# First feed-forward stage of an eight-stage kernel: side work dealt out anew over the four chunks of a unit

## What is computed

```python
def _L0_ffn_ref(x, Wg, ln_scale, ln_bias, W1, b1, W2, b2):   # x is _layernorm(x)
    logits = xt @ Wg.T
    top1 = jnp.argmax(logits, axis=-1)
    xhat = (xt - mu) * jax.lax.rsqrt(var + LN_EPS)
    def body(y, p):
        h = jax.nn.gelu((xhat * s_e + b_e) @ w1 + bb1, approximate=False)
        out = h @ w2 + bb2
        mask = (top1 == eid)[:, None].astype(out.dtype)
        return (y + mask * out, None)
```

## Time and profile before

| | us |
|---|---|
| median of 3 runs | 3491.15 |
| lowest, highest | 3480.52, 3493.16 |
| profiled execution, device time | 3460.41 |
| its span, first to last instruction | 3458.1 |
| the stage `f0`, first up step to the last combine | about 388 to 541 |

### The profile page before, as it was taken

How to read it: one execution, slowest core, us unless ns; L and a number is a source line. 1 busy time by engine, 2 the same in 40 slices (tenths; PEclk the granted TensorE clock), 3 DMA queues, 4 the chain that set the end, 5 groups by cost and what they waited for, 6 DMA issues and landing times. The chain is left out here.

```text
span 3458.1 us, 70868 instructions
## 1 busy us (share of the span) xinstructions
PE 2853.0 (83%) x26206; PEld 1911.0 (55%) x26206; DVE 2008.3 (58%) x4613; ACT 1670.4 (48%) x3112; POOL 1267.8 (37%) x1503
## 2 busy tenths in 40 slices
PE   5888576888879999999969889999209977999993
PEld 3544354445436666666645556666209865777772
DVE  4777454787655444443358777777724335555647
ACT  3777332666634444444337666666315533333331
POOL 6554005777300000000055455653260035555533
PEclk8999797999979999999979999999559978999995
DMA  3221002111124000000011111111142333333211
GB/s 112 70 70 58 13 1 75 61 63 61 33 66 159 1 1 1 1 1 1 6 56 60 61 48 39 43 45 31 41 167 87 93 98 85 81 84 83 65 29 49
DMA packets 211341, 190.00 MB, mean 55 GB/s; under 512 B 41840, under 2 KB 189568, under 8 KB 210848
## 3 DMA queue, kind: packets, MB, share of 16 engines
q1 hardware_dynamic: 184384, 167.44, 16.0%
q0 software_dynamic: 26624, 18.04, 2.0%
HBM read 67.09 MB, written 41.42 MB: 31 GB/s over the span
## 5 line engine op out<-in xcount | busy, mean ns | idle before, releaser
L1545 DVE TENSOR_TENSOR f1H<-f1HF,f1H 128x512 bf16<-128x512 f32 x256 | 176.6, 692 | 398.3 <-ACT f1H L1390 398.3
L1323 PE MATMUL ps<-f1xT,f1w 128*128 128x512 bf16 x1536 | 378.3, 383 | 6.1 <-ACT f1H L1390 6.1
L1345 PE MATMUL ps<-f1w,f1H 128*128 128x256 bf16 x3072 | 378.6, 273 | 0.0
L1345 PEld LDWEIGHTS ps<-f1w,f1H 128*128 128x128 bf16 x3072 | 301.0, 98 | 90.9 <-issue 1.1
L1387 ACT ACTIVATE f1HF<-ps 128x512 f32<-128x512 f32 x256 | 152.8, 597 | 333.9 <-PE ps L1323 333.8
L734 ACT ACTIVATE a2PT<-ps 128x512 f32<-128x512 f32 (+1 forms) x512 | 262.3, 542 | 100.9 <-PE ps L573 56.0
L430 POOL DMA_DIRECT2D a2QS<-a2MH x256 | 135.5, 535 | 289.1 <-DVE a2MH L959 276.4
L550 PE MATMUL ps<-a2KS,a2QS 49*128 49x256 bf16 (+1 forms) x1024 | 182.5, 269 | 69.4 <-DVE a2NM L853 24.5
L1323 PEld LDWEIGHTS ps<-f1xT,f1w 128*128 128x128 bf16 x1536 | 147.9, 98 | 151.1 <-issue 16.4
L1233 POOL TENSOR_TENSOR f1RS<-f1VE,neghalf 128x4 f32<-128x4 f32 x8 | 8.1, 1012 | 541.5 <-DVE f1VE L1528 541.5
L853 DVE TENSOR_REDUCE a0NM<-ps 128x2 f32<-128x512 f32 x256 | 166.2, 684 | 53.1 <-PE ps L550 52.8
(11 more groups left out here) (512 smaller groups left out, 7266.3 us busy)
## 6 DMA issues: line engine op xcount, KB each, us to landing
a2KS<-a2KH SPq DMA_DIRECT2D x192, 64.0 KB
a2QS<-a2QH SPq DMA_DIRECT2D x192, 64.0 KB, 2.6
a4KS<-a4KH SPq DMA_DIRECT2D x96, 128.0 KB
a4QS<-a4QH SPq DMA_DIRECT2D x96, 128.0 KB, 2.6
slots<-zeros SPq DMA_DIRECT2D x1, 9984.0 KB, 32.4
f2XS<-slots SPq DMA_DIRECT2D x39, 256.0 KB, 2.9
results<-f2XS SPq DMA_DIRECT2D x39, 256.0 KB, 2.1
f1WF<-in_f_w SPq DMA_DIRECT2D x32, 256.0 KB, 2.7
```

The source lines that it names most:

```text
L1323: m = nc.tensor.matmul(ps[:, (u * NCH + i) % 2, :], w1[:, x, kt, i * P:i * P + P], xT[:, half, y, kt, :], start=(j == 0), stop=(j == len(t ...
L1345: m = nc.tensor.matmul(out, H[:, (u * NCH + i) % HR, x, t * P:t * P + P], w2[:, y, i, :], start=first, stop=(f == YC - 1 and j == 2 and no ...
L1545: nc.vector.tensor_tensor(H[:, (u * NCH + i) % HR, 1, :], HF[:, (u * NCH + i) % 2, :], H[:, (u * NCH + i) % HR, 0, :], SUB).then_inc(S["h_ ...
```

## The change

In `f0` the side work of a unit is dealt out over its four chunks in another way:

| after chunk | before | after |
|---|---|---|
| 0 | xT 0 | xT 0, xT 1 |
| 1 | xT 1, route | route, gate |
| 2 | stats, gate | stats |
| 3 | apply, sel | sel, apply |

xT, route, gate and sel are those of the next unit, stats and apply those of the unit after it. In addition the four DVE multiplications of the ties by a triangular mask (L1443, one per tile) become one over all four tiles. The order of `f1` stays as it was.

```diff
         def early(u, k):
-            k = k if paired else k // 2
+            if paired:
+                if u + 1 < UNITS:
+                    yield from ((("xT", u + 1, 0), ("xT", u + 1, 1)), (("route", u + 1, 0), ("gate", u + 1, 0)),
+                                (), (("sel", u + 1, 0),))[k]
+                if u + 2 < UNITS and k >= 2:
+                    yield ("stats" if k == 2 else "apply", u + 2, 0)
+                return
+            k = k // 2
...
                 if u + 2 < UNITS:
                     yield ("apply", u + 2, 0)
-                if u + 1 < UNITS and paired:
-                    yield ("sel", u + 1, 0)
...
                     link(nc.vector.tensor_tensor(EQ[:], every, own, ALU.is_equal))
-                    for t in range(UT):
-                        v = nc.vector.tensor_tensor(EQ[:, t], EQ[:, t], g["tri"][:, 0:NE, 0:E], MUL)
-                    link(v)
+                    if NE == E:
+                        lower = g["tri"][:, 0:NE, 0:E]
+                        link(nc.vector.tensor_tensor(EQ[:], EQ[:], lower.rearrange("p (one n) e -> p one n e", one=1
+                                                                                 ).to_broadcast([P, UT, NE, E]), MUL))
+                    else:
+                        for t in range(UT):
+                            v = nc.vector.tensor_tensor(EQ[:, t], EQ[:, t], g["tri"][:, 0:NE, 0:E], MUL)
+                        link(v)
```

## The result

The changed kernel takes 3463.43 us (median of 12 runs, 3454.3 to 3478.7), the kernel before 3493.27 us (12 runs, 3475.4 to 3507.6). The ratio is 0.9928, with a 95% interval from 0.9906 to 0.9949: 25 us, or 0.7%, faster (18 to 33 us by the interval). The two medians by themselves are 29.8 us apart, but a median moves by some us with the runs that happen to be in it, so I go by the ratio. Forecast were 31 us and 3460 us.

What follows compares the result with a forecast made beforehand. PE bounds the stage, stalled mainly by the gate chain behind stats. Units of 15.3 us for 20.28 give 27.7 us, unit 0 3.0, the first chain 0.2: 30.9 off 3491.15, so 3460 us, range 3444 to 3480.

Steps and rivals of the forecast that it cites:

- What bounds the stage: PE bounds the stage; its largest stall is waiting for the gate chain behind stats, 2.84 us ahead of sel.
- the sum: Stage gain: 27.7 us over six units of 15.3 us, 3.0 in unit 0, 0.2 ahead of the first: 30.9 us.
- the last combine: Sign at the stage's end in the profile of after: last combine near 510 in place of 540.
- Gate ahead of stats: On DVE, the gate chain ends at 12.85, PE reaches sel at 14.81: no wait, 1.9 us to spare.
- xT 1 right behind xT 0: On PE, sharing bank 6 adds a bare wait of 1.60 us; xT 1 starts 2.03 us after xT 0.
- The mask: In DVE's gate chain, one multiplication priced 0.42 us for 0.63; the chain takes 2.65 us instead of 2.85.
- Stats and apply: Behind gate on DVE, apply just fits before the next unit's xT 0: 0 to 0.1 us late, no slack left.
- rival 2: DVE late with apply or gate chain: 1 us in six units, 3466 us, at the outside 3480; chance 0.10.
- Unit 0: The stage's first unit: the 2.83 us ahead of unit 1's sel go, with the down step's end: 3.0 back.
- The clock: After the sel stall goes, its half-clock stretch goes too: 1.7 us a unit back, the bare wait costing none.
- Rival 1: The bare wait between xT 0 and xT 1 drops the clock: 1.7 us a unit, 19 back, 3472; chance 0.13.

Runs made afterwards that it cites:

- e3: Changed kernel with xT 1 moved back behind chunk 1, ahead of route: stage 135.7 us, against 129.1 for the changed kernel.
- e4: Changed kernel with gate moved back behind stats, both xT still behind chunk 0: stage 149.75 us.
- e1: Kernel before, old order, with only the one mask multiplication in place of four: stage 154.8 us, against 154.5.
- e2: Changed kernel's new order with the old four mask multiplications: stage 135.7 us, against 129.1.
- e9: Changed kernel again, unedited, timed in a second series: ratio 0.9927 (0.9913 to 0.9941), stage 128.75 us.
- e5: Changed kernel with DVE holding chunk 3's H subtraction back until POOL's power is done: stage 135.5 us.
- e7: Changed kernel with stats behind chunk 0 and apply behind chunk 2, one PSUM bank for both xT: stage 125.5 us.
- e8: Changed kernel with xT 1 in PSUM bank 7, stats behind chunk 0 and apply behind chunk 2: stage 112.4 us.
- e12: The e8 kernel again, unedited, now timed: 3441.3 us against 3485.0 for the kernel before, ratio 0.9879.
- e11: Kernel before, profiled once more, unedited: stage 156.5 us, against 154.5 in its first profile.

## Why the prediction was right, and where it was not

*What bounds the stage: right.* PE was held by the gate chain behind stats, and when that moved, the stage shortened by 25.4 us, all of which is found in the whole time (25 us by the ratio). Forecast were 30.9, so 3460 us lies closer to the measured 3463.43 than the sum deserves: some 4 us of the 29.8 between the medians are not in the stage, and that is luck. Of the last combine, which ended at 520.4 and not near 510, 4.2 us are the later start of the stage in this profile (391.29 for 387.07), and the rest is what follows here.

*Gate ahead of stats: right.* Sel waits in no unit but the first; e3 and e4 show that this move carries the gain, each by leaving out one of the two moves.

*xT 1 right behind xT 0: right within 0.2 us in the full units.* The wait is 1.50 us by the brackets, 1.92 in unit 0, and xT 1 starts 462.19 - 460.03 = 2.16 us after xT 0, where I had 2.03.

*The mask: right by its length.* It takes 0.42 us, and e1 and e2 both show 0.2 us a unit where its chain is bare. That it may keep drops of the clock away, I did not think of.

*Stats and apply: the mechanism right, the size off.* I named apply as what is late next, and took 0 to 0.1 us. It is 0.34 us late: up 0 and a down step take 460.03 - 456.87 = 3.16 us up to xT 0 and not 2.82. It was the power at 1.38 us, not 1.01, that added the 0.3: I had checked that DVE's H subtraction fits beside the power and took both at the length they had apart. With the 0.13 us above a unit is 15.75 us and not 15.3, and unit 1 is 16.04: over six units 503.68 - 408.89 = 94.8 us and not 91.8, 3.0 us less gain. This is rival 2 in its small form.

*Unit 0: off by 2.4 us, by the clock.* I carried unit 0 at the pace it had before and 3.0 us back; 0.6 came back in the first profile. In e9 the 3.0 us came, and unit 1 lost 2.1. Together, 30.9 - 3.0 - 2.4 leaves 25.5; measured are 25.4 in the stage and the 0.2 ahead of the first sel, 25.6.

*The clock: the forecast came true for a reason that does not hold, and that was luck.* I argued that a pause of 1.72 us had left the clock at full in six units (the earlier trace rows shows one of them; the trace has all six so) and so one of 1.6 us would. e3 has the same 1.72 us pause with a drop in all six full units, e2 and e5 have the 1.50 us pause with four drops in six each, and e4 has a 2.63 us pause without a drop three times. So the six units of the kernel before, whose pauses recur every 20.28 us, were closer to one sample than to six. The changed kernel's five quiet units, 15.75 us apart, may be just such a sample, or they are quiet because hardly anything stands ahead of their bare wait; three profiles agree on them, and e7's six units say the same. Rival 1 was real at a price of 1.5 to 2.1 us each time, and its chance was worth more than the 0.13 I gave it; it happened at most once a stage and not seven times. Why the drop chooses the units that it does is open: I made no run that shifts the pauses alone.

## What to carry to other kernels

When side work is dealt out over the chunks of a loop, put the longest serial chain that a later step needs first on its engine, and what has slack behind it; then lay out one unit by the rows and look for the step with no slack left, since that is the one to have a term wrong. Give two transposes in a row two banks: it was a small edit here, and took 14 us more off the stage. A short pause of TensorE costs more than its length some of the time, and two close behind each other did so more often here than one, so compare two orders by their sum of steps and by several profiles, not by one.

## What the runs showed that I had not expected

**A power on GpSimd, 128x4, takes 1.01 us alone and 1.38 us beside a VectorE subtraction of 128x512** with two SBUF inputs that starts ahead of it.

**Half clock after a pause is not a matter of the pause's length alone**, between 1.5 and 2.7 us: pauses of 1.50, 1.72 and 2.63 us were each seen with a drop and without one. The 1.50 us pause had one in 10 of 15 units where a wait of 0.23 us or more came ahead of it, and in 0 of 27 where that wait was 0.17 us or less.

**The last attention stage has two lengths.** From its first to its last normalisation on POOL it took 443 to 447 us in the first profile before and in e1 to e4, and 463 to 474 us in all other profiles, of either order. e1 to e4 were run one after the other on one chip, and the kernel before took 3455 us beside them; beside e5 to e8, on another chip, it took 3483, and beside e9 to e12, on a third, 3485. The first line is the kernel before, the second e11, the same kernel (starts of first and last):

```profile
L442 POOL TENSOR_SCALAR a4XN<-X,a4MV,a4RS x32: 1209/1220/1232, 2830.8 to 3274.2; 128x256 f32<-128x256 f32 x32
```
```profile
L442 POOL TENSOR_SCALAR a4XN<-X,a4MV,a4RS x32: 1208/1220/1232, 2831.7 to 3295.5; 128x256 f32<-128x256 f32 x32
```

These 20 us are most of the 31 by which the first profile before lay under its runs, and why the spans of the two first profiles hide the change. Its cause is open: no run was aimed at it, and a difference between chips or sessions was not told apart from others.
